# Attention keys' first half loaded after its last step, and the next group's maxima moved eight scores forward

## The reference

```python
q, k, v = jnp.split(x @ c_attn_w + c_attn_b, 3, axis=-1)      # 16 heads of 16
scores = jnp.einsum('bhqd,bhkd->bhqk', q, k) * scale
scores = jnp.where(causal, scores, -inf)
weights = jax.nn.softmax(scores, axis=-1)
attn = jnp.einsum('bhqk,bhkd->bhqd', weights, v)
```

## Time and profile before

| what | us |
|---|---|
| median of 3 runs | 3241.5 (3239.0 to 3245.0) |
| the profiled execution's own time | 3248.3 |
| its span | 3246.6 |
| one period of the attention | 133.0 |
| mean granted clock of PE | 0.931 |

### The profile page before, as it was taken

The page is one execution under the profiler, slowest core; times in us unless marked ns, Lnnn a source line. Parts: engine busy times, 40 slices in busy tenths (PEclk is TensorE's granted clock), DMA queues, the critical chain, the costliest instruction groups (busy, mean ns, idle before and its releaser), DMA issues.

```text
span 3246.6 us, 44876 instructions
## 1 busy us (share of the span) xinstructions
PE 2866.4 (88%) x14054; PEld 1312.8 (40%) x14055; DVE 2118.9 (65%) x2956; ACT 1441.0 (44%) x2500; POOL 1274.6 (39%) x1473
## 2 busy tenths in 40 slices
PE   6888888898888988889999998788899899999976
PEld 4555423233233232256666665663222232232222
DVE  7776576676666766022222222554999999999997
ACT  4521456565565655711212121425445545545442
POOL 3330122111221112200000001845888888898885
PEclk9999999898898988989999999888899899998988
DMA  6783404313132132031111112630000000000000
GB/s 208 205 158 117 131 16 69 50 27 58 30 59 47 27 48 69 25 92 29 32 31 31 31 31 57 221 122 7 1 14 20 1 20 20 1 20 13 1 13 20
DMA packets 175049, 176.37 MB, mean 54 GB/s; under 512 B 50666, under 2 KB 151533, under 8 KB 174765
## 3 DMA queue, kind: packets, MB, share of 16 engines
q1 hardware_dynamic: 168748, 157.52, 19.6%
q0 software_dynamic: 6144, 16.82, 1.6%
HBM read 100.46 MB, written 73.83 MB: 54 GB/s over the span
## 4 chain that ended last, share of the span: by engine, by line
PE 53%; DVE 17%; issue 9%; POOL 9%; ACT 4%; DMA 2%; another core or an unknown queue 1%; SPq 1%; POOLq 0%; DVEq 0%; ACTq 0%
PE ps L1752 50%; DVE hh L1718 6%; POOL Ch L934 5%; DVE mp L1479 5%; DVE ps L1705 2%; PE ps L2005 2%; DMA qk<-qk_parts 1%; ACT Pt L1084 1%; DVE tl L1695 1%; ACT dA L1264 1%; POOL dt L900 1%; POOL dtx L894 1%; PE ps L1953 1%; POOL dtx L903 1%
## 5 line engine op out<-in xcount | busy, mean ns | idle before, releaser
L1479 DVE TENSOR_REDUCE mp<-ps 128x1 f32<-128x1024 f32 (+7 forms) x768 | 669.3, 909 | 287.5 <-PE ps L1752 260.0
L1084 ACT ACTIVATE Pt<-ps 128x512 f32<-128x512 f32 (+3 forms) x1280 | 611.7, 539 | 386.5 <-PE ps L1752 356.0
L1752 PE MATMUL ps<-qk 99*128 99x512 bf16 (+7 forms) x2560 | 646.1, 364 | 114.1 <-DVE mp L1479 62.8
L934 POOL TENSOR_TENSOR Ch<-hh,Cb 128x1024 f32<-128x1024 f32 x256 | 603.3, 2359 | 40.9 <-DVE hh L1718 40.9
L792 POOL TENSOR_SCALAR_AFFINE_SELECT Pt<-Pt 128x128 f32<-128x128 f32 x512 | 146.5, 292 | 904.0 <-ACT Pt L1084 896.8
L1718 DVE TENSOR_TENSOR_SCAN hh<-dA,hst,ps 128x512 f32<-128x512 f32 x384 | 473.0, 1262 | 0.0
L1752 PEld LDWEIGHTS ps<-qk 99*128 99x128 bf16 (+1 forms) x2560 | 214.0, 100 | 582.0 <-DVE mp L1479 216.6
L1264 ACT ACTIVATE dA<-ps 128x1024 f32<-128x1024 f32 x256 | 261.6, 1022 | 356.4 <-PE ps L1752 356.0
L1752 PE MATMUL ps<-dtx,pick 32*128 32x512 f32 x1024 | 325.0, 685 | 74.3 <-DVE hh L1718 73.5
L1705 DVE TENSOR_TENSOR ps<-ps,Bb 128x512 f32<-128x512 f32 x512 | 325.6, 681 | 28.4 <-PE ps L1752 28.0
L1752 PE MATMUL ps<-dt,WA 32*128 32x512 f32 x1024 | 321.0, 705 | 15.6 <-ACT dA L1264 14.6
(11 more groups left out here) (306 smaller groups left out, 3526.0 us busy)
## 6 DMA issues: line engine op xcount, KB each, us to landing
qk<-qk_parts SPq DMA_DIRECT2D x192, 128.0 KB, 5.7
W<-in_L_ffn_w SPq DMA_DIRECT2D x16, 1024.0 KB, 10.8
qk_parts<-q SPq DMA_DIRECT2D x32, 384.0 KB, 3.0
expert_out<-yb SPq DMA_DIRECT2D x72, 128.5 KB, 2.5
expert_in<-zero SPq DMA_DIRECT2D x9, 1024.0 KB, 10.4
xg<-expert_in SPq DMA_DIRECT2D x72, 128.0 KB, 2.7
X<-in_L_attn_x SPq DMA_DIRECT2D x2, 2048.0 KB, 10.2
x_rows<-x2h SPq DMA_DIRECT2D x8, 512.0 KB, 5.9
```

The costliest lines, as they stand in the source:

```text
L934: pool.tensor_tensor(Ch[:, k % 6, :, :], hh[:, k % HRING, :, :], Cb[:, par:par + 1, :].broadcast_to([P, 2, CH]), ALU.mult).then_inc(s_Ch, 1)
L1084: act.activation(Pt[:, n % PRING, q0:CH], ps[:, 4 + n % SRING, q0:CH], ACT.Exp, scale=SCALE).then_inc(s_exp, 1)
L1479: dve.tensor_reduce(mp[:, qc, h, t % TPC, k0 // 1024:k0 // 1024 + 1], slot[:, 0:n], AX.X, ALU.max).then_inc(s_free, 1)
L1752: return pe.matmul(o, lhsT, rhs, start=start, stop=stop, **kw)
```

## The change

Three things change in stage 2, and nothing elsewhere.
- `LATE` goes from 10 to 2, and `SPARE = 8` is new: the 100 units of maxima are spread over scores 2 to 151 at the same rate, and none lies among the last eight scores.
- The first half of the keys of group g+2 is loaded when step 31 is done (`KEYS_STEP`), the last one that reads key tiles 0 to 7. SP's place for it is ahead of ring unit 89 (`KEYS_FREE`), the first behind `pv 31` in the plan.
- The remaining 12 DMAs (second halves) stay at the end of the period.

```diff
--- before.py
+++ after.py
@@ -123,7 +123,7 @@
 DIAGONAL = [n for n in range(NE) if EU[n][2] >= TPC * EU[n][1]]
 ND = len(DIAGONAL)
 SRING, PRING = 3, 8
-LATE = 10
+LATE, SPARE = 2, 8
 LAST_STEP = [max(n // HG for n in range(NE) if EU[n][1] == qc) for qc in range(CPB)]
 
 
@@ -140,7 +140,7 @@
             if step in LAST_STEP:
                 late.append((n + 6, LAST_STEP.index(step)))
 
-        while with_max and n >= LATE and m * (NE - LATE) < NM * (n + 1 - LATE):
+        while with_max and n >= LATE and m < NM and m * (NE - LATE - SPARE) < NM * (n + 1 - LATE):
             out.append(MU[m])
             m += 1
         if late and late[0][0] == n:
@@ -159,6 +159,8 @@
 
 FULL_PLAN, FIRST_PLAN, LAST_PLAN = period_plan(True, True), period_plan(False, True), period_plan(True, False)
 NR = len(ring_of(FULL_PLAN))
+KEYS_STEP = max(n // HG for n in range(NE) if EU[n][2] < QT // 2)
+KEYS_FREE = len(ring_of(FULL_PLAN[:FULL_PLAN.index(("pv", KEYS_STEP)) + 1]))
 
 
 UNITS = KI * 8
@@ -572,6 +574,9 @@
                     sp.wait_ge(s_vg, g + 1)
                     load_v(g + 1)
                 for r, u in enumerate(ring_of(plan)):
+                    if stack and r == KEYS_FREE:
+                        sp.wait_ge(s_pv, g * STEPS + KEYS_STEP + 3)
+                        load_stack(g + 2, par, 1, 0)
                     if u[0] == "turn":
                         store_max(g + 1, 1 - par, u[1])
                     if u[0] == "back":
@@ -582,7 +587,8 @@
                             load_stack(g + 2, par, 0, 0)
                 if stack:
                     sp.wait_ge(s_pv, (g + 1) * STEPS + 2)
-                    load_rest(g + 2, par)
+                    load_stack(g + 2, par, 0, 1)
+                    load_stack(g + 2, par, 1, 1)
 
             load_group(1, 1)
             load_v(0)
```

## The result

The changed kernel took 3206.8 us (median of 4 runs, 3200.4 to 3210.7), against 3243.0 for the kernel before (4 runs). The ratio is 0.9888, 95% interval 0.9868 to 0.9907: 36 us less, where the prediction said 15 less, with 0.5 to 31.5 as its range. Its profiled execution took 3205.7 us, with a span of 3204.0.

A forecast was written before the change was run, and what follows sets the result against it. PE's own work was taken to bound the kernel, leaving its idle and half-clock time to win. 22 us won at period starts less 7 lost at ends gave 15 less: 3226 us from 3241.5, range 3210 to 3241.

The forecast's parts named there:

- What bounds the kernel: Attention: PE's own work sets the 133.0 us period; winnable are 15.2 us of idleness and the time at half clock.
- The load: Behind step 31: 6 DMAs issue some 26 us before the next period in 2.9 us, nothing late; the wait goes.
- The price of the wait: At the first maximum: the load wait costs 5.1 us, 3.4 of waiting and 1.7 of work at half clock.
- The bound from period 0: Score 0 to score 16 took 9.29 us there, against 14.41: at most 5.1 us a period, 31 us in all.
- The start of the period: Score 0 to 16, now with nine maxima, takes 11.5 us instead of 14.41: 3.7 us a period won, 22 us in all.
- The end of the period: From score 152, without maxima: nothing won; a clock falling after the turn's wait loses 1.0 us at seven ends, 7 us.
- Moving a maximum wins nothing by itself.: Attention: shifting maxima between places gains nothing, since PE's own work sets the period.
- The rule that stood against the change: By it all seven period ends would run at half clock, leaving 7 us less in total instead of 15.
- A: Clock holds through the period's end and comes back at once: 22 to 31 us less, 3210 to 3219; chance 0.22.
- B: Clock falls at every turn: ends cost 15.4 us, starts give 22, 6.8 us less, 3235; chance 0.15.
- C: Slower: PE at half clock from the turn's wait at score 150 to beyond score 16, 5 us more, 3247; chance 0.09.
- D: The wait stays, as another load or the ring's slot ends last at score 2: 3242 to 3249 us; chance 0.04.

The follow-up runs named there:

- y1: Changed kernel with the maxima back on scores 10 to 159, so the early load alone, on a chip of the 3200 us kind: 3166.2 us, 0.9898 of before.
- z0: The kernel before, unchanged, traced in a later session on a chip where it takes about 3200 us: 3198.0 us, ratio 1.0003.
- x3: Changed kernel with its maxima spread over scores 2 to 159, so the last eight scores have theirs: 3155.6 us, 0.9862 of before.
- x1: Changed kernel with the maxima back on scores 10 to 159, so the early load alone, in an earlier session: 3163.4 us, 0.9885 of before.
- y0: The changed kernel itself (scores 2 to 151), run beside three other plans on one chip: 3160.8 us, 0.9880 of before.
- z1: Kernel before with 18 unread matmuls ahead of each period's first wait for the stack loads: 3193.6 us, 0.9984 of before.
- y3: Changed kernel with its maxima on scores 2 to 159, run beside three other plans on one chip: 3157.7 us, 0.9870 of before.
- z2: Changed kernel with maxima on scores 2 to 159 and 6 unread matmuls in the wait for the last turn: 3138.3 us, 0.9811 of before.
- y4: Changed kernel with its maxima on scores 10 to 151, the densest plan: 3194.0 us, 0.9983 of before.
- the plan by cost: Changed kernel with maxima laid out by their cost instead of their number, from score 2 to the end: 3145.1 us, 0.9829 of before.
- x6: Changed kernel with 6 unread matmuls in PE's wait for the last turn: 3204.4 us, 0.9877 of before.
- w1: The plan by cost with unread matmuls in the wait for the last turn: 3143.7 us, 0.9832 of before.
- w2: Kernel before with only 6 unread matmuls in the wait for the last turn: 3193.7 us, 0.9985 of before.
- x5: Kernel before with 8 unread matmuls ahead of each period's first wait for the stack loads: 3196.0 us, 0.9990 of before.

## Why the prediction was wrong

*What bounds the kernel.* Right: PE with its waits and its clock. The wait for the loads was the target and is gone.

*The load.* Right in every part: issued behind step 31, some 25 us early, 6 DMAs in 2.74 us, nothing late. The price of the wait was right as well, as far as the profile gave it. The bound from period 0, 5.1 us a period and 31 us in all, is about what the load alone gave: 34 us by y1, and 5.2 us a start by the timelines of z0 and y1.

*The start of the period.* This step failed. I took 3.7 us and not 5.1 as won, since I had six of the maxima done at half the clock until 8 us behind the transposes, as in period 7. Score 0 to score 16 took 8.43 us on average, not 11.5, and 14.52 before: 6.1 us less, and 6.9 with the 0.8 for the five maxima, so 41 us in six periods where I had 22. Even my upper bound was too low, and the reason is that it had a fall of the clock in it: periods 0 and 7 pass that stretch at 0.64 and 0.60, so neither was a stretch at the full clock. In the changed kernel two of the six starts are at 1.00 throughout (8.07 us each) and none is below 0.81. (I also took the clock to be back within 7 us in both; by its 0.60 over 9.3 us it was 7.4 in period 7.) Whether the maxima themselves bring the clock back is not shown. For it speaks that on one chip it is down for 6.8 us behind each turn of x3 but the last, and for 6.8 or 10.2 behind those of x1; the two plans differ in the density of the maxima as well.

*The end of the period, and the sum.* This step failed too, by less in itself. I charged 7 us for a clock that falls ahead of nine narrow scores. It fell ahead of them at three ends of seven and cost 3.7 us there. The shift in fact left the clock higher, not lower: 0.99 against 0.96 (y0, y1), 14.0 us less of busy time in six periods for the same matmuls. That the clock has this price is shown by z1, and that filling the turn's wait keeps it up in the plan of y3 by z2; both change nothing but what PE does in a wait. The early start does it with either end (y3 against y1, y0 against y4); the empty end alone does not, since y4's clock is below y1's. Why with both together so many falls are gone is open. The wait for the turn, which I left at 1.95 us, is 1.78.

*"Moving a maximum wins nothing by itself."* Too simple, and a term that I had put at nothing. The shift costs 9.6 us of idle time (y0, y1) where the sum has none, and wins more in busy time; the same 100 units on scores 10 to 151 lose 28 us against scores 10 to 159 (y4, y1). I had not looked at DVE's share of single stretches: by the mean of a period of about 121 us DVE has 30 us of slack (y1, y0), from `back 0` to `back 1` it has 4.5 with the load alone (23.20 less 18.74) and 4.0 with the shift.

*The rule that stood against the change.* The Trainium skill ("TensorE: Matmul & The Clock Gate", section "A second HAM failure mode: psum-queue depth-cycling") has the clock go down and up with frequent short pauses between groups of matmuls. I had given it a small chance on the evidence of period 7. This case agrees in part: in x3 and y3 the clock fell behind a wait of 1.79 us at all seven ends, and filling that wait took every fall in the six periods away in z2 (clock 1.00). But in the changed kernel it fell ahead of the transposes at three of seven ends with the same wait, not at all seven as I had the rule say.

*The rivals.* A, the clock holds and comes back at once, was the nearest, with a chance of 0.22 and 22 to 31 us; it holds for the ends without a fall. B happened at three ends of seven. C and D did not happen. My range ended at the upper bound of A, since I had let the shift only cost.

*Open:* what makes PE stand still near score 109 on some chips, 6 us a period; why the clock falls behind some turns and not behind others with the same wait; and why the plan by cost has more waits for DVE.

## What to carry to other kernels

Price a wait of PE by a stretch of the same trace in which it does not occur, clock and all, and take that number as the estimate rather than as the upper bound, if the clock in it is no lower than it will be in yours. Where PE waits a microsecond or two for another engine at a fixed place, try a few matmuls that nobody reads in the wait: in the best plan here that was worth 16 to 19 us by the ratios of z2, x3 and y3, taken on three chips (9 to 13 in the six periods of their traces), and in two others nothing that was clear of noise (x6, w1). And judge how densely a second stream of work may lie by the other engine's busy share in each stretch between two events, not by its mean.

## What the runs showed of the hardware

- The granted clock fell behind PE's wait for the turn at seven ends of seven in the kernel before (1.95 us) and in x3 and y3 (1.79 us), and in the changed kernel (1.78 us) ahead of the transposes at three of seven and with the next scores at a fourth. In w2, where that wait is filled, it was down from 862.5 to 865.9, ahead of a wait of 4.19 us for loads, and again from 869.4 on, within it. In x5 it rose during filler work and fell again behind a wait of 1.86 us.
- A few matmuls that are never read, put in one wait of each period, held the clock at 1.00 over 706 us (z2), without lengthening the period.
- The kernel before takes 3198 to 3200 us on some chips and 3243 to 3247 on others, medians. Over six periods the difference is 37.4 us (798.09 less 760.68): 21.8 of idle time, a pause in each period at the same place of the program, and 15.6 of busy time, with the clock at 0.50 for 6.8 us behind the pause. The changed kernel has the pause too on such chips, in several pieces.
